# A graph network on one core: signals between the engines per lot of pairs, not per pair

## The reference

```
agg = segment_sum(x[src], dst);  h = MLP((1 + eps) * x + agg)                 # gin
for l in range(2):                                                           # attention
    g = h @ W;  e = leaky_relu(s[src] + d[dst]);  alpha = softmax of e over the edges of each dst
    h = segment_sum(g[src] * alpha, dst) + bias      # with a loop edge at every node
alpha = softmax over (dst, type) of score(xl[src, type] + xr[dst, type] + e_feat), 4 heads, 4 types
agg = segment_sum(xl[src, type] * alpha, (dst, type)); mean over heads, mix of types, ffn  # relational
out = relu(segment_sum((x @ W)[src] * norm, dst) + b)                         # gcn
```

## Time and profile before

| | us |
|---|---|
| median of three runs | 10306.99 |
| lowest, highest | 10287.10, 10349.91 |
| profiled execution, device time | 10344.3 |
| its span, first to last instruction | 10342.5 |

### The profile page before, as it was taken

The page is one execution under the profiler, slowest core; times in us unless marked ns, Lnnn a source line. Parts: engine busy times, 40 slices in busy tenths (PEclk is TensorE's granted clock), DMA queues, the critical chain, the costliest instruction groups (busy, mean ns, idle before and its releaser), DMA issues. The chain is left out here.

```text
span 10342.5 us, 94979 instructions
## 1 busy us (share of the span) xinstructions
PE 5314.2 (51%) x23667; PEld 3474.6 (34%) x23667; DVE 5146.7 (50%) x19201; ACT 1901.7 (18%) x4679; POOL 5637.5 (55%) x5712
## 2 busy tenths in 40 slices
PE   2333413333332333337877778778767777623333
PEld 2223312222231222233322222222237777522322
DVE  3233433333342333348677777777766666632325
ACT  0000011111111111111022222222234444400000
POOL 6666235455526555531266666666656666366663
PEclk7555655555565555568989899989988888855555
DMA  2111021121221121216766667666656666211111
GB/s 63 47 46 47 22 51 51 54 57 49 57 50 49 55 57 50 55 40 252 297 204 206 204 204 212 203 205 204 208 155 176 178 178 178 82 51 47 46 47 34
DMA packets 433882, 1155.67 MB, mean 112 GB/s; under 512 B 105716, under 2 KB 147156, under 8 KB 420424
## 3 DMA queue, kind: packets, MB, share of 16 engines
q0 software_dynamic: 295984, 849.83, 28.6%
q1 hardware_dynamic: 122892, 275.14, 7.8%
q10 hardware_dynamic: 14476, 24.62, 0.7%
HBM read 1016.65 MB, written 132.52 MB: 111 GB/s over the span
## 5 line engine op out<-in xcount | busy, mean ns | idle before, releaser
L813 POOL DMA_INDIRECT gat_ring<-gat_table,psrc_idx x1664 | 1600.8, 962 | 1796.2 <-PE bank L866 731.8
L566 DVE TENSOR_TENSOR acc<-acc,bank 128x129 f32 (+1 forms) x1664 | 479.3, 288 | 1534.2 <-remote 836.3
L866 PE MATMUL bank<-gat_ring,gat_hot 128*128 128x130 f32 x3328 | 730.0, 385 | 975.6 <-DVE gat_hot L971 574.1
L982 DVE TENSOR_TENSOR acc<-acc,bank 128x130 f32 x1664 | 482.0, 290 | 1285.4 <-remote 696.0
L1735 POOL DMA_INDIRECT pair<-right_table,idx_r_idx x782 | 796.0, 1018 | 551.3 <-issue 188.6
L1885 POOL DMA_INDIRECT msg<-left_table,pidx_idx x832 | 810.3, 974 | 481.0 <-issue 197.2
L1735 POOL DMA_INDIRECT acc<-left_table,idx_l_idx x782 | 802.0, 1026 | 434.6 <-issue 219.9
L866 PEld LDWEIGHTS bank<-gat_ring,gat_hot 128*128 128x128 f32 x3328 | 622.1, 275 | 1077.2 <-DVE gat_hot L971 572.4
L512 POOL DMA_INDIRECT gcn_sum_ring<-gcn_table,src_idx x782 | 762.6, 975 | 381.2 <-issue 226.2
L512 POOL DMA_INDIRECT gin_sum_ring<-in_x,src_idx x782 | 759.0, 971 | 372.9 <-issue 221.2
L1774 PE MATMUL bank<-pair,ident 128*128 128x512 f32 x1564 | 870.2, 640 | 0.0
(11 more groups left out here) (533 smaller groups left out, 9516.9 us busy)
## 6 DMA issues: line engine op xcount, KB each, us to landing
gat_place<-local_rows SPq DMA_DIRECT2D x128, 416.0 KB
left_table<-rel_out SPq DMA_DIRECT2D x49, 1032.0 KB, 4.9
right_table<-rel_out SPq DMA_DIRECT2D x49, 1032.0 KB, 3.9
feat<-attr_rows SPq DMA_DIRECT2D x194, 256.0 KB
gat_ring<-gat_table,psrc_idx POOLq DMA_INDIRECT x1664
types<-type_rows SPq DMA_DIRECT2D x98, 256.0 KB
msg<-left_table,pidx_idx POOLq DMA_INDIRECT x832
gin_sum_ring<-in_x,src_idx POOLq DMA_INDIRECT x782
```

The costliest lines, as they stand in the source:

```text
L813: e.indirect_dma_start(ring[:, at:at + TROW], None, table[:, :], bass.IndirectOffsetOnAxis(ap=ed["psrc"][:, i:i + 1], axis=0)).then_inc(*g ...
L866: e.matmul(k.psum[i % NBANK][:, 0:TROW], hot[i // HQ % NH][:, i % HQ * P:(i % HQ + 1) * P], ring[:, at:at + TROW], start=True, stop=True). ...
```

## The change

In the gin and gcn sums and in the attention layers a lot is HQ = 4 pairs, in rel_sum PAIR = 2. Within a lot an engine works without signals and raises its semaphore with the last instruction: `product`, `added`, `scaled`, in rel_sum also `hot_made`, `scaled_v` and `scaled_s`. The adds of one lot still follow each other by a semaphore of DVE's own (`chained`). Banks hold two products each, in three double banks (NP2 = 3, 12 pairs) in the sums and attention and in five banks (10 pairs) in rel_sum. DVE makes the hot tiles of lot i and then adds lot i - 1 (in rel_sum lot i - 2), in place of a lag of three pairs. In rel_sum NS goes from 5 buffers of one pair to 3 of two. POOL's waits keep their places and count lots. In `aggregate_rows`, PE's register load stands before the wait for the hot tiles.

```diff
@@ aggregate_rows
-        NQ, Q, NH, NBANK = 22, HQ, 3, 6
+        NQ, Q, NH, NP2, NBATCH = 22, HQ, 3, 3, PAIRS // HQ
+        sums = lambda b, n: k.psum[2 * (b % NP2) + n // 2][:, n % 2 * 256:n % 2 * 256 + width]
@@ gpsimd
-                        e.wait_ge(*product.at(free))
+                        e.wait_ge(*product.at(-(-free // Q)))
@@ tensor
-                for j in range(PAIRS):
-                    b = j // Q
-                    if j % Q == 0:
-                        if j < TILES:
-                            e.wait_ge(*got[b % NQ].at(b // NQ * Q + size(b), 16))
-                        e.wait_ge(*hot_made.at(b + 1))
-                    if j % BATCH == 0:
-                        at = k.regs(ENG.PE, ed["ring_row"], j, BATCH, (RING - 1) * TROW)
-                    if j >= NBANK:
-                        e.wait_ge(*added.at(j - NBANK + 1))
-                    e.matmul(k.psum[j % NBANK][:, 0:width], hot[b % NH][:, j % Q * P:(j % Q + 1) * P],
-                             ring[:, bass.ds(at[j % BATCH], width)], start=True, stop=True).then_inc(*product.up())
+                for b in range(NBATCH):
+                    if b * Q < TILES:
+                        e.wait_ge(*got[b % NQ].at(b // NQ * Q + size(b), 16))
+                    if b * Q % BATCH == 0:
+                        at = k.regs(ENG.PE, ed["ring_row"], b * Q, BATCH, (RING - 1) * TROW)
+                    e.wait_ge(*hot_made.at(b + 1))
+                    if b >= NP2:
+                        e.wait_ge(*added.at(b - NP2 + 1))
+                    for n in range(Q):
+                        m = e.matmul(sums(b, n), hot[b % NH][:, n * P:(n + 1) * P],
+                                     ring[:, bass.ds(at[(b * Q + n) % BATCH], width)], start=True, stop=True)
+                    m.then_inc(*product.up())
@@ vector: hot tile of lot i, then the adds of lot b = i - 1
+                        e.wait_ge(*product.at(b + 1))
+                        for n in range(Q):
+                            into = acc[:, bass.ds(at[(b * Q + n) % BATCH], width)]
+                            add = e.tensor_tensor(into, into, sums(b, n), ALU.add)
+                            if b or n:
+                                add.wait_op(*(chained if n else added).now(), "sem-ge")
+                            add.then_inc(*(added if n == Q - 1 else chained).up())
@@ gat_edges (tensor; gpsimd and vector change as above)
-                    for i in range(lo, lo + CT):
-                        if i % HQ == 0:
-                            e.wait_ge(*hot_made.at(i // HQ + 1))
-                        e.wait_ge(*scaled.at(i + 1))
-                        if i >= NBANK:
-                            e.wait_ge(*added.at(i - NBANK + 1))
-                        at = i % (2 * CT) * TROW
-                        e.matmul(k.psum[i % NBANK][:, 0:TROW], hot[i // HQ % NH][:, i % HQ * P:(i % HQ + 1) * P],
-                                 ring[:, at:at + TROW], start=True, stop=True).then_inc(*product.up())
+                    for q in range(lo // HQ, (lo + CT) // HQ):
+                        e.wait_ge(*hot_made.at(q + 1))
+                        e.wait_ge(*scaled.at(q + 1))
+                        if q >= NP2:
+                            e.wait_ge(*added.at(q - NP2 + 1))
+                        for n in range(HQ):
+                            at = (q * HQ + n) % (2 * CT) * TROW
+                            m = e.matmul(sums_of(q, n), hot[q % NH][:, n * P:(n + 1) * P], ring[:, at:at + TROW], start=True,
+                                         stop=True)
+                        m.then_inc(*product.up())
@@ gat_edges (scalar)
-                    for i in range(cn * CT, (cn + 1) * CT):
-                        row = ring[:, i % (2 * CT) * TROW:i % (2 * CT) * TROW + F + 1]
-                        e.mul(row, row, wt[:, i % CT:i % CT + 1]).then_inc(*scaled.up())
+                    for q in range(cn * CT // HQ, (cn + 1) * CT // HQ):
+                        for i in range(q * HQ, (q + 1) * HQ):
+                            row = ring[:, i % (2 * CT) * TROW:i % (2 * CT) * TROW + F + 1]
+                            m = e.mul(row, row, wt[:, i % CT:i % CT + 1])
+                        m.then_inc(*scaled.up())
@@ rel_sum
-        NG, NS, NBANK, FIX, FETCH, TURN = 15, 5, 5, 24, 72, 100
+        NG, NS, NBANK, FIX, FETCH, TURN = 15, 3, 5, 24, 72, 100
-        hot = [k.sb(f"rhot{j}", P, ctx=late) for j in range(NS)]
-        hotw = [soft.val, soft.top, soft.ex, soft.same, soft.step]
+        hot = [k.sb(f"rhot{j}", PAIR * P, ctx=late) for j in range(NS)]
+        hotw = [(soft.val, soft.top), (soft.ex, soft.same), (soft.step, soft.pen)]
@@ rel_sum (tensor)
+                    e.wait_ge(*scaled_v.at(j + 1))
+                    e.wait_ge(*scaled_s.at(j + 1))
+                    for n in range(PAIR):
+                        for h in range(H):
+                            m = e.matmul(k.psum[j % NBANK][:, n * F:(n + 1) * F], hotw[j % NS][n][:, h * P:(h + 1) * P],
+                                         rows[j % NG][:, n * LROW + h * F:n * LROW + (h + 1) * F], start=(h == 0),
+                                         stop=(h == H - 1))
                     m.then_inc(*product.up())
@@ rel_sum (vector): lot i is made, lot i - 2 is added
```

More of the change, by code:

```diff
@@ L965, in sums @@
                 def sums(cn):
-                    for i in range(cn * CT, (cn + 1) * CT + LAG):
-                        if i < (cn + 1) * CT and i % HQ == 0:
-                            q = i // HQ
-                            if q >= NH:
-                                e.wait_ge(*product.at((q - NH + 1) * HQ))
+                    first, ends = cn * CT // HQ, (cn + 1) * CT // HQ
+                    for i in range(first, ends + 1):
+                        if i < ends:
+                            if i >= NH:
+                                e.wait_ge(*product.at(i - NH + 1))
@@ L977, in sums @@
+                        q = i - 1
+                        if q < first:
                             continue
-                        if j % HQ == 0:
-                            at = k.regs(ENG.DVE, ed["acc_row"], j, HQ, (NB - 1) * ROW)
-                        e.wait_ge(*product.at(j + 1))
-                        into = acc[:, bass.ds(at[j % HQ], ROW)]
-                        add = e.tensor_tensor(into, into, k.psum[j % NBANK][:, 0:ROW], ALU.add)
-                        add.wait_op(*(added.now() if j % CT else ready.now()), "sem-ge").then_inc(*added.up())
+                        at = k.regs(ENG.DVE, ed["acc_row"], q * HQ, HQ, (NB - 1) * ROW)
@@ L985, in _ @@
+                        e.wait_ge(*product.at(q + 1))
+                        for n in range(HQ):
+                            into = acc[:, bass.ds(at[n], ROW)]
+                            add = e.tensor_tensor(into, into, sums_of(q, n), ALU.add)
+                            before = chained if n else added if q > first else ready
+                            add.wait_op(*before.now(), "sem-ge").then_inc(*(added if n == HQ - 1 else chained).up())
                 for t, v in ((acc, 0.0), (step, -BIG), (met, -BIG), (rest, -BIG)):
@@ L1990, in _ @@
-                    j = i - LAG
-                    if j >= 0:
-                        if j % BATCH == 0:
-                            at = k.regs(ENG.DVE, ed["acc_row"], j, BATCH, (NB - 1) * ROW)
-                        e.wait_ge(*product.at(j + 1))
-                        into = acc[:, bass.ds(at[j % BATCH], F)]
-                        add = e.tensor_tensor(into, into, k.psum[j % NBANK][:, 0:F], ALU.add)
-                        add.wait_op(*(added.now() if j else filled.at(1)), "sem-ge").then_inc(*added.up())
+                        mine = ed["local"][:, i * PAIR:(i + 1) * PAIR]
@@ new lines, in _ @@
+                        m.then_inc(*scaled_v.up())
+                    b = i - 2
+                    if b >= 0:
+                        if b * PAIR % BATCH == 0:
+                            at = k.regs(ENG.DVE, ed["acc_row"], b * PAIR, BATCH, (NB - 1) * ROW)
+                        e.wait_ge(*product.at(b + 1))
+                        for n in range(PAIR):
+                            into = acc[:, bass.ds(at[(b * PAIR + n) % BATCH], F)]
+                            add = e.tensor_tensor(into, into, k.psum[b % NBANK][:, n * F:(n + 1) * F], ALU.add)
+                            before = chained.now() if n else added.now() if b else filled.at(1)
+                            add.wait_op(*before, "sem-ge").then_inc(*(added if n == PAIR - 1 else chained).up())
```

104 lines of the change are left out of this document (48 added, 56 removed).

## The result

The changed kernel takes 10,205.05 us (median of 4 runs, 10,189.52 to 10,217.33); the kernel before 10,308.61 us (also 4 runs: one measured beside it, and the three of the table above). The ratio is 0.9879 with a 95% interval of 0.9855 to 0.9903: faster by 1.2%, where the forecast was 9,500 us, 8% faster. The direction was right, the size was not. (More than half of the later runs were on chips of another kind, where the kernel before takes 8,427 us, as the experiments tell.)

What follows compares the result with a forecast made beforehand. The prediction took late PE-to-DVE hand-offs beside POOL's gathers as the bound. Its terms, -305 (sums), -300 (attention) and -200 (messages), sum to -805 us: 10344 - 805 = 9539, or 9,500 us, range 9,100 to 10,450.

Steps and rivals of the forecast that it cites:

- What bounds the kernel: Whole kernel: no engine over 55% busy; hand-offs decide, PE's completions reaching DVE late while POOL gathers; about 6300 of 10342 us.
- Its ring is full most of the time: POOL's gathers: POOL idles 1796 us before L813, so the PE-DVE loop is the slower of the two.
- The two readings: PE's completions beside gathers: lateness comes either with each signal or with each instruction; the forecast hangs on which.
- late per signal: PE to DVE beside gathers: each signal is delayed, so fewer signals help; rel_sum's adds wait 2.44 us, the next follows 0.92 us on.
- the 1.41 us: Attention weights, L836: small matmuls, 13 to a signal, start 1.41 us apart beside gathers; used for the weights' slow pace.
- 1, sums: Gin and gcn sums: one signal per four pairs lets POOL set the pace; -148 and -157 us, bounds -305 and 0.
- 2, attention: Attention layers: sums shrink to 26 to 35 us, weights grow, 85 us a chunk; -300 us, bounds -876 and +42.
- The +42 us for filling: Sums and attention: DVE's first add waits for four pairs rather than one, 1.3 us in each of 32 chunks.
- 3, messages: rel_sum: halved signals and ten pairs of banks halve the 429 us idle before adds; -200 us, bounds -229 and 0.
- 4, POOL at no cost: Register loads, added waits and POOL's waits rounded to the lot cost nothing, covered by waits for product.
- Nothing gained: Rival for the whole kernel: lateness goes by instruction, 1.40 us a pair stays; 10,340 us, chance 0.18.
- Slower: bursts bring on the crawl: Rival: lots of 16 loads and matmuls without waits crawl at 1.41 us each beside gathers; 10,700 us, chance 0.20.

Runs made afterwards that it cites:

- signal by matmul: Changed kernel, but each matmul of the sums and attention layers raises product again, waits staying per lot: 10,168 us.
- matmuls twice: Changed kernel with each matmul of the sums and attention layers issued twice, with its weight load, signals unchanged: 10,395 us.
- half the instructions: Changed kernel with products of sums and attention from the upper 16 bits, one load and one matmul a pair: 10,152 us on chip 1.
- gathers late: Changed kernel, but POOL waits for a whole chunk's products before refilling the attention ring: 10,479 us on chip 1, ratio 1.0157 to the kernel before.
- lockstep: Changed kernel with TensorE waiting, before each lot of sums and attention, for the previous lot's adds: 10,524 us, ratio 1.0196 to the kernel before.
- plain transfers: Changed kernel with attention's indirect gathers replaced by plain POOL transfers of 128 consecutive rows: 8,868 us on chip 3, 8,874 us on chip 1.

## Why the prediction was wrong

Cycles on slowing chips side by side (us); "alone" is the cycle less POOL's 65, "done beside" is own work less alone:

| kernel | sums | weights | cycle | own work | alone | done beside gathers |
|---|---|---|---|---|---|---|
| before, chip 1 | 65.7 | 30.7 | 97.1 | 54.1 | 32.1 | 22 |
| changed | 62.9 | 29.8 | 93.1 | 53.0 | 28.1 | 25 |
| signal by matmul | 62.9 | 30.1 | 91.7 | 52.9 | 26.7 | 26 |
| matmuls twice | 68.8 | 28.6 | 97.6 | 58.3 | 32.6 | 26 |
| half the instructions | 53.3 | 39.3 | 93.0 | 51.3 | 28.0 | 23 |
| gathers late | 25.7 | 74.3 | 103.0 | 53.0 | 38.0 | 15 |
| lockstep | 70.6 | 27.4 | 97.7 | 75.1 | 32.7 | 42 |
| plain transfers | 25.5 | 27.4 | 52.9 | 52.9 | | |

In the first five kernels of the table the loop does 22 to 26 us of its own work in the 65 us in which POOL issues indirect gathers, with a signal per pair or per lot and with half or twice the instructions; the rest is done while POOL stands at a full ring. The cycle is then 65 + (own work - some 25). That is the table's last column turned round, not a second proof, and it is no law: with the gathers beside the weights only 15 us are done (by 25 the cycle would be 93, not 103), and lockstep does 42, probably since nearly half of its own work is waiting for DVE, which can lie beside the hold. What holds TensorE inside stays open: no row names it.

By the prediction's own points:

- **What bounds the kernel.** Right: hand-offs, slow beside gathers alone, against the rule of the Trainium skill ("SBUF — State Buffer", section "SBUF: two separate sides") that TensorE never waits on anyone. On chips 7, 9 and 10 the traces agree with that rule (25.5 us beside 19 gathers), on 1 and 3 they do not. That a second kind of chip exists could not be seen from one trace. What could be seen, and was not read, is the mean pace in attention: four pairs of one chunk beside gathers took 4.99 us on average before (4.89 after), and four of POOL's gathers take 5.00. There the loop was slow in bouts, but on the whole as fast as POOL. In gin's sums it was not: four pairs took 5.6 us. Two readings were loose. "Its ring is full most of the time" took all of POOL's 1796 us idle before L813; 732 of them end with a product and 153 are "remote", while 470 are pauses of issue and 442 two waits of POOL's own queue. And gathers come 1.25 us apart, not 1.27; the 0.30 us of issue is in the trace, but not in the earlier trace rows.
- **The two readings: the step that failed.** The whole sum rested on "late per signal": that the slow arrivals, "some 3 to 4 us each", keep that size when one signal stands for four pairs, and so stay under POOL's 5.1 us a lot. Measured: the "remote" waits became 6.7 us each in attention and 10.0 in the sums (1207.8 / 121), and were 2.4 to 2.7 times fewer., which I read as proof for it, come from a stage with little lateness: from first to last gather of the messages it is 1.54 us a pair there and 1.30 on chip 9, pair by pair on both. The earlier trace rows had spoken against it, and I left them with the rival. But the 1.41 us in them, from which I worked out how slowly the weights pass, is a single distance: between the starts within the groups of 13 the mean is 0.14 us in that trace, for starts are when matmuls are handed over, not when they are done.
- **What the lateness is worth was sized well.** Pair by pair on chip 9, where there is none, gin's matmuls last 933 us from first to last, gcn's 1018, the messages' gathers 1085, against 1066, 1169 and 1280 on the slowing chip: 133, 151 and 195 us less, for the -148, -157 and -200 of the sum. Lots were to bring what only the other kind of chip brings.
- **1, sums: -305 us taken, -17 measured** (-13 and -4). Gin's last gather was to end at 1044 us; it started at 1146.3, where it had started at 1146.4.
- **2, attention: -300 taken, -120 measured.** Both terms failed: the sums stayed at 62.9 us instead of 26 to 35, and so the weights did not grow (29.8). That they would have grown was right: to 39.3 and 74.3 us on chip 1 when lateness or gathers were shifted there. (The 41.4 us on chip 7 are another thing: there TensorE waits for rows.) The +42 us for filling are there, but outweighed: without gathers the first add comes 1.3 us later in its chunk, and the rest of the sums is 2.3 us shorter. So they fell from 26.7 to 25.6 us, which in 32 chunks is some 33 us saved; the rest of the 120 is 22 against 25 us done beside gathers, whose cause is open.
- **3, messages: -200 taken, -6 measured**, by the same failed step.
- **4, POOL at no cost:** true on slowing chips, where POOL waits anyway. On the others POOL's gathers became longer, and the kernel is 0.6 to 0.7% slower.
- **The rivals.** "Nothing gained" came nearest in time (10,340), but its reason, lateness by instruction, is refuted by doubling, and by halving as far as the cycle goes. "Slower: bursts bring on the crawl" is refuted by the changed kernel's own time and by doubling (bursts twice as long, no more lateness); lockstep excludes running ahead. Of the two bounds kept for attention, -876 and no gain, the measured -120 lies near the second.

A version that beats both kernels was not found. Attention in lots with the sums and messages left alone avoids most of the +0.6% (1.001) on unslowed chips and should keep -120 us on slowing ones; the latter is an inference from stage lengths.

## What to carry to other kernels

When a loop is slow only beside another engine's work, find out first what in that work the lateness goes with: change its kind (here plain for indirect transfers, -1,340 us, with other rows summed) before changing the hand-over, whose form moved 1%. Multiply the mean wait by its count before and after: here a third as many waits were 2.6 times as long. Compare the loop's mean pace with the neighbour's pace (4.99 against 5.00 us in attention), and sum whole cycles, since time taken out of one stage may come back in the next.

## What the runs showed of the hardware

- The same kernel before takes 8,418 to 8,438 us on chips 7, 9 and 10 and 10,305 to 10,333 us on chips 1 and 3 (one set of runs on each), with gathers at the same 1.25 us and the clock of the weights at 1.2 GHz (0.50) on both. Where the changed kernel's traces of both kinds were compared, the difference lies beside indirect gathers, in late results of TensorE: 62.9 against 25.7 us for 52 pairs, and 14.2 against 0.77 us for three small products with the gathers beside the weights. Without gathers the sums take 25.6 us on both, and the stretch after gcn's last matmul 71.5 and 71.6 us.
- An indirect gather of 128 rows kept POOL busy for 982 ns and came every 1.25 us; a plain transfer of the same bytes 541 ns, and TensorE was not held beside it.
- Signals of TensorE had no visible price: 624 more in each layer and sum, and the cycle was 91.7 against 93.1 us (one trace each).
